# Eight transformer layers with linear attention on one core: the second norm on VectorE, the four gelu chunks together, and bias rows added by GpSimd instead of TensorE

## The reference

```
q = elu(h @ wq + bq) + 1;  k = elu(h @ wk + bk) + 1;  v = h @ wv + bv
kv = sum over tokens of k (x) v, per head;  z = 1 / (q . sum(k) + 1e-6)
att = (q . kv) * z
h = ln(h + att @ wo + bo) * g1 + be1
y = gelu(h @ w1 + c1) @ w2 + c2          # 512 hidden columns
h = ln(h + y) * g2 + be2
```

## Time and profile before

| | us |
|---|---|
| median of three runs | 1039.72 |
| the profiled execution | 1038.53 |
| its span, first to last instruction | 1036.6 |
| busy: PE / ACT / DVE / POOL | 950.8 / 777.6 / 750.1 / 301.4 |
| granted TensorE clock, mean of the span | 0.967 |

### The profile page before, as it was taken

The page is one execution under the profiler, slowest core; times in us unless marked ns, Lnnn a source line. Parts: engine busy times, 40 slices in busy tenths (PEclk is TensorE's granted clock), DMA queues, the critical chain, the costliest instruction groups (busy, mean ns, idle before and its releaser), DMA issues.

```text
span 1036.6 us, 18947 instructions
## 1 busy us (share of the span) xinstructions
PE 950.8 (92%) x5782; PEld 755.7 (73%) x5782; DVE 750.1 (72%) x2466; ACT 777.6 (75%) x1333; POOL 301.4 (29%) x299
## 2 busy tenths in 40 slices
PE   3569999999899998999899998999899999999980
PEld 2447887778777887778777886788777887787650
DVE  6867777777677767677677767677677778778646
ACT  2457888888788887888788887888788888888622
POOL 5103222322233222232233222232223222345513
PEclk9879999999999999999999999999999999999965
DMA  4100100000000100001000100001000000000002
GB/s 143 54 9 15 36 1 1 19 6 32 1 18 0 36 1 0 18 0 35 1 18 0 36 1 0 18 0 35 1 17 1 0 0 2 1 1 2 1 0 81
DMA packets 22440, 16.67 MB, mean 16 GB/s; under 512 B 3964, under 2 KB 18280, under 8 KB 22376
## 3 DMA queue, kind: packets, MB, share of 16 engines
q1 hardware_dynamic: 22376, 16.00, 5.2%
HBM read 13.89 MB, written 2.10 MB: 15 GB/s over the span
## 4 chain that ended last, share of the span: by engine, by line
PE 66%; ACT 13%; DVE 12%; issue 7%; DVEq 0%; DMA 0%; POOL 0%; POOLq 0%; ACTq 0%
PE down_ps L639 17%; PE q_ps L598 6%; PE q_ps L580 5%; PE k_ps L574 5%; ACT z_tm L767 4%; ACT L794 4%; PE att_ps L610 3%; PE up_ps L627 3%; PE up_ps L629 3%; PE up_ps L628 3%; PE small_ps L587 3%; DVE st L821 3%; PE t_ps L617 3%; PE small_ps L592 3%; PE down_ps L635 3%
## 5 line engine op out<-in xcount | busy, mean ns | idle before, releaser
L639 PEld LDWEIGHTS down_ps<-w_use,hid 128*128 128x128 f32 x2048 | 243.2, 192 | 44.9 <-issue 44.9
L639 PE MATMUL down_ps<-w_use,hid 128*128 128x128 f32 x2048 | 255.8, 278 | 0.0
L709 ACT ACTIVATE hid<-up_ps 128x512 f32<-128x512 f32 x256 | 144.8, 589 | 70.7 <-PE up_ps L629 64.5
L860 POOL TENSOR_TENSOR res_ffn<-z_tm,g_ffn 128x512 f32<-128x512 f32 x64 | 104.7, 1635 | 302.9 <-DVE z_tm L842 302.9
L853 POOL TENSOR_TENSOR res_att<-z_tm,g_att 128x512 f32<-128x512 f32 x64 | 82.4, 1288 | 351.4 <-DVE h L809 351.3
L816 DVE TENSOR_TENSOR h<-down_ps,res_ffn 128x512 f32<-128x512 f32 x64 | 44.2, 691 | 112.7 <-ACT z_tm L767 112.7
L821 DVE BATCH_NORM_STATS2 st<-h 128x6 f32<-128x128 f32 x512 | 110.9, 279 | 2.2
L627 PE MATMUL up_ps<-z_hi,w_hi 128*128 128x512 f32 x256 | 111.9, 437 | 0.4 <-DVE gate_bc L488 0.3
L767 ACT ACTIVATE z_tm<-h,shift,rstd 128x128 f32<-128x128 f32 x256 | 105.6, 483 | 2.9 <-DVE shift L834 2.1
L629 PE MATMUL up_ps<-z_lo,w_hi 128*128 128x512 f32 x256 | 101.6, 397 | 0.0
L628 PE MATMUL up_ps<-z_hi,w_lo 128*128 128x512 f32 x256 | 100.5, 393 | 0.0
(11 more groups left out here) (170 smaller groups left out, 1755.4 us busy)
## 6 DMA issues: line engine op xcount, KB each, us to landing
raw_w<-in_L_attn_W SPq DMA_DIRECT2D x16, 256.0 KB, 4.7
x_tm<-in_L_attn_x SPq DMA_DIRECT2D x4, 512.0 KB, 5.9
bias_bc<-in_L_attn_c SPq DMA_DIRECT2D x8, 256.0 KB, 4.3
out_y<-gate_tm SPq DMA_DIRECT2D x8, 256.0 KB, 2.0
raw_g<-in_L_attn_g SPq DMA_DIRECT2D x15, 64.0 KB
raw_att<-in_L_attn_Wq SPq DMA_DIRECT2D x8, 64.0 KB, 1.8
raw_att<-in_L_attn_Wk SPq DMA_DIRECT2D x8, 64.0 KB, 1.8
raw_att<-in_L_attn_Wv SPq DMA_DIRECT2D x8, 64.0 KB, 1.9
```

Source lines behind the costliest of these rows:

```text
L639: last = nc.tensor.matmul(down_ps[:, t, :], hid[:, j, t * P:(t + 1) * P], w2_use[:, j, :], start=False, stop=(j == FC - 1 and t == TT - 1))
L709: nc.scalar.activation(hid[:, j, :], up_ps[j % 2][:, :], ACT.Gelu).then_inc(s["gelu"], 1)
L860: nc.gpsimd.tensor_tensor(res_ffn[:, b % 2, :, :], z1_tm[:, :, :], g_ffn[:, :].unsqueeze(1).to_broadcast([P, TT, D]), ALU.mult).then_inc(s ...
```

## The change

There are six edits, and they depend on each other:

1. **Bias rows.** The two 2 x 512 matmuls go, with the split of the rows. The rows are now loaded by DMA to all 128 partitions. POOL adds them itself: `res_att` and `res_ffn` are each a multiply and then an add in place, so POOL has four 128 x 512 operations a period in place of two.
2. **When POOL works.** `res_att` of unit p is released by `mv1_s`, the aggregated statistics of unit p-1, no longer by `h1_s`. `res_ffn` is done for unit p-2 in period p, one period later than before, behind `res_att`, and has one buffer in place of two.
3. **Second norm.** `act_norm2` goes; `dve_norm2` does the same four instructions on DVE.
4. **DVE's order.** Both sets of `bn_stats` come first and both of `bn_aggr` after; the second half is norm1, k_phi, kvo, q_n, z1_lo, norm2, q_phi, h2.
5. **Up chunks together.** `pe_up` runs its four chunks in one piece, the third into the bank of `k_ps`, before `pe_kz`; the projection of k follows `pe_kz`.
6. **Down by tiles.** `pe_down` goes token tile by token tile with the four chunks inside, in three pieces: one tile before the denominator, one after, two after the projection of q. It waits for all four gelus.

```diff
         def pool_res_att(pool, u, b):
             z_ready(pool, u)
             if after_first(u):
-                pool.wait_ge(s["h1_s"], u)
+                pool.wait_ge(s["mv1_s"], TT * u)
             nc.gpsimd.tensor_tensor(res_att[:, :, :], z_tm[:, b, :, :], g_att[:, :].unsqueeze(1).to_broadcast([P, TT, D]),
-                                    ALU.mult).then_inc(s["t2m"], 1)
+                                    ALU.mult).then_inc(s["t2x"], 1)
+            pool.wait_ge(s["t2x"], u + 1)
+            nc.gpsimd.tensor_tensor(res_att[:, :, :], res_att[:, :, :], row_att[:, :].unsqueeze(1).to_broadcast([P, TT, D]),
+                                    ALU.add).then_inc(s["t2m"], 1)
         def pool_res_ffn(pool, u, b):
-            if after_first(u) and after_first(u - 1):
-                pool.wait_ge(s["h2_s"], u - 1)
+            if after_first(u):
+                pool.wait_ge(s["h2_s"], u)
             pool.wait_ge(s["z1n"], TT * (u + 1))
-            nc.gpsimd.tensor_tensor(res_ffn[:, b % 2, :, :], z1_tm[:, :, :], g_ffn[:, :].unsqueeze(1).to_broadcast([P, TT, D]),
-                                    ALU.mult).then_inc(s["t1m"], 1)
+            nc.gpsimd.tensor_tensor(res_ffn[:, :, :], z1_tm[:, :, :], g_ffn[:, :].unsqueeze(1).to_broadcast([P, TT, D]),
+                                    ALU.mult).then_inc(s["t1x"], 1)
+            pool.wait_ge(s["t1x"], u + 1)
+            nc.gpsimd.tensor_tensor(res_ffn[:, :, :], res_ffn[:, :, :], row_ffn[:, :].unsqueeze(1).to_broadcast([P, TT, D]),
+                                    ALU.add).then_inc(s["t1m"], 1)
...
-            if is_unit(p - 1):
-                pool_res_ffn(pool, p - 1, (b - 1) % SEQS)
+            if is_unit(p - 2):
+                pool_res_ffn(pool, p - 2, (b - 2) % SEQS)
...
         def pe_att(pe, u):
-            nc.tensor.matmul(att_flat, ones_r[:, :], row_att[:, :, :].rearrange("p t d -> p (t d)"), start=True, stop=False)
...
+        up_bank = (up_ps[0][:, :], up_ps[1][:, :], k_ps[:, :, :].rearrange("p t d -> p (t d)"), up_ps[0][:, :])
+        def pe_up(pe, u, keys):
+            pe.wait_ge(s["z1lo_s"], u + 1)
+            if after_first(u):
+                pe.wait_ge(s["gelu"], u * FC)
+            for j in range(FC):
+                if j == 2:
+                    pe.wait_ge(s["kphi"], keys)
+                if j == 3:
+                    pe.wait_ge(s["gelu"], u * FC + 1)
...
+        def pe_down(pe, u, tiles):
+            if tiles[0] == 0:
                 if after_first(u):
                     pe.wait_ge(s["h2_s"], u)
-                nc.tensor.matmul(down_flat, ones_r[:, :], row_ffn[:, :, :].rearrange("p t d -> p (t d)"), start=True, stop=False)
...
+                pe.wait_ge(s["gelu"], u * FC + FC)
+            for t in tiles:
+                for j in range(FC):
...
-        def act_norm2(act, p, v, b):
-            act.wait_ge(s["shift_s"], p)
...
+        def dve_norm2(dve, p, b):
+            dve.wait_ge(s["shift_s"], p)
+            for t in range(TT):
+                i = TT + t
+                nc.vector.tensor_scalar(z_tm[:, b, t, :], h2[:, t, :], rstd[:, i:i + 1], shift[:, i:i + 1],
+                                        ALU.mult, ALU.add).then_inc(s["z2n"], 1)
```

More of the change, by code:

```diff
@@ L111, in build @@
         res_att = sb("res_att", [P, TT, D])
-        res_ffn = sb("res_ffn", [P, 2, TT, D])
+        res_ffn = sb("res_ffn", [P, TT, D])
         h1 = sb("h1", [P, TT, D])
@@ L609, in pe_att @@
             for t in range(TT):
-                last = nc.tensor.matmul(att_ps[:, t, :], q_n[:, t * P:(t + 1) * P], kvo[:, :], start=False, stop=(t == TT - 1))
+                last = nc.tensor.matmul(att_ps[:, t, :], q_n[:, t * P:(t + 1) * P], kvo[:, :], start=True, stop=True)
             last.then_inc(s["att_done"], 1)
@@ L618, in pe_z1_transpose @@
             last.then_inc(s["t1_ps"], 1)
-        def pe_up(pe, u, chunks):
-            if chunks[0] == 0:
-                pe.wait_ge(s["z1lo_s"], u + 1)
-            for j in chunks:
-                if after_first(u) or j >= 2:
-                    pe.wait_ge(s["gelu"], u * FC + j - 1)
-                w_hi, w_lo = w1_hi[:, j * P:(j + 1) * P], w1_lo[:, j * P:(j + 1) * P]
-                nc.tensor.matmul(up_ps[j % 2][:, :], w_hi, z1_hi[:, :], start=True, stop=False)
-                nc.tensor.matmul(up_ps[j % 2][:, :], w_lo, z1_hi[:, :], start=False, stop=False)
-                nc.tensor.matmul(up_ps[j % 2][:, :], w_hi, z1_lo[:, :], start=False, stop=True).then_inc(s["up"], 1)
@@ L639, in pe_down @@
                     last = nc.tensor.matmul(down_ps[:, t, :], hid[:, j, t * P:(t + 1) * P], w2_use[:, j, :],
-                                            start=False, stop=(j == FC - 1 and t == TT - 1))
-            if chunks[-1] == FC - 1:
+                                            start=(j == 0), stop=(j == FC - 1))
+            if tiles[-1] == TT - 1:
                 last.then_inc(s["down"], 1)
@@ L761, in act_z1_hi @@
             nc.scalar.activation(z1_hi[:, :], t_ps[:, :], ACT.Identity).then_inc(s["z1hi_s"], 1)
-        def act_norm2(act, p, v, b):
-            act.wait_ge(s["shift_s"], p)
-            for t in range(TT):
-                i = TT + t
-                nc.scalar.activation(z_tm[:, b, t, :], h2[:, t, :], ACT.Identity, scale=rstd[:, i:i + 1],
-                                     bias=shift[:, i:i + 1]).then_inc(s["z2n"], 1)
         def act_state_copy(act, u, b):
@@ L815, in dve_h2, with dve_stats_of @@
                 dve.wait_ge(s["z2n"], TT * u)
-            nc.vector.tensor_tensor(h2[:, :, :], down_ps[:, :, :], res_ffn[:, b % 2, :, :], ALU.add).then_inc(s["h2_s"], 1)
-        def dve_norm_stats(dve, h, first, ready, count, st_s, mv_s, done):
+            nc.vector.tensor_tensor(h2[:, :, :], down_ps[:, :, :], res_ffn[:, :, :], ALU.add).then_inc(s["h2_s"], 1)
+        def dve_stats_of(dve, h, first, ready, count, st_s):
             dve.wait_ge(ready, count)
@@ L821, in dve_norm_stats, with dve_aggr_of @@
                 nc.vector.bn_stats(st[:, first + t, :], h[:, t, :]).then_inc(s[st_s], 1)
+        def dve_aggr_of(dve, first, st_s, mv_s, done):
             dve.wait_ge(s[st_s], TT * done + TT)
@@ L1036, in _ @@
                     load_a(sp, l)
[L1037 removed]
+                    sp.wait_ge(s["w2_ready"], l)
                     load_b(sp, l)
@@ L1138, in _ @@
                 pe_expert_up(pe, 0)
-                pe_up(pe, last, range(FC))
+                pe_up(pe, last, UNITS)
                 pe_expert_down(pe, 2)
```

151 lines of the change are left out of this document (70 added, 81 removed).

## The result

| kernel | median us | lowest to highest | runs |
|---|---|---|---|
| before | 1041.49 | 1038.48 to 1046.07 | 4 |
| changed | 1128.63 | 1123.47 to 1131.88 | 4 |

The ratio is 1.0828, with a 95% interval of 1.0765 to 1.0891: slower by 87 us. The profiled execution took 1130.56 us.

The account below looks back on a forecast made before the run. PE bound the kernel before; a DVE-POOL-DVE ring would bound the changed one at 14.8 us a period. Six looped layers add 51 us, layer 0 5, layer 7 5 and 14, draining 3: 78 on 1038.5, forecast 1117, range 1085 to 1143.

Parts of the forecast that it names:

- The mechanism: Norm1 on DVE waits for POOL's four operations, which wait for h1's statistics; ordinary periods of 14.6 to 15.0 us; chance 0.88.
- the ring: DVE's h1 addition and statistics, POOL's four operations, then DVE to the next h1 addition: 14.6 us a period, floor 14.4.
- a second ring, through PE and ACT: From norm1 through PE and ACT to k_phi and the next h1 addition: 29.5 us for two periods, 14.75 each.
- The term for b = 2: Period b = 2 of a layer: the w2 copy between POOL's pairs adds 0.6 us.
- The clock: PE's clock falling from 2.4 to 1.2 GHz in new gaps within layers would put the time far above the range.
- b = 3: Period b = 3: small operations for the next layer's affines about 0.7 us, plus POOL's row work about 1.5.
- the loop's turn, b = 7: Period in which the hardware loop turns: 2.7 us extra, on DVE and so in the ring.
- Layer 7: Last layer: four periods of 17.6 us against 14.2, adding 14; its four ordinary-like periods add 5.
- PE stays the bound: Rival, whole kernel: norm1 not held by POOL, PE sets 13.15 us a period, total 988 us; chance 0.04.
- the doubling of terms that I had put to this rule: DVE and POOL blocking on their shared port could double the b = 1 and layer 7 terms: 12 us more.

Follow-up runs that it names:

- e1: Changed kernel with POOL's two res_ffn operations ahead of its two for res_att, the w2 copy staying between the pairs; 1066.13 us.
- e3: Changed kernel with POOL's product into res_att released by the h1 addition instead of the statistics behind it; 1043.57 us.
- e11: Changed kernel with res_att released by the h1 addition and, at b = 2, the w2 copy ahead of the res_att pair; 1019.77 us.
- e2: Changed kernel with only the w2 copy of period b = 2 moved ahead of POOL's res_att pair; 1093.80 us.
- e5: Changed kernel with five small matmuls of constants put into TensorE's wait ahead of the z1 transposes; 1106.93 us.
- e12: Kernel before with only the second norm moved from ScalarE to VectorE; 1001.14 us.
- e15: Kernel before, its engine order kept, with second norm on VectorE, bias rows on GpSimd, no bias matmuls, two res_ffn buffers; 976.70 us.

## Why the prediction was right, and where its steps were off

**The mechanism was right.** The time lies in the range, 12 us above the predicted 1117. The signs of the mechanism are in the trace: norm1 released by POOL's in-place addition, POOL's four operations back to back, PE idle 1.75 to 1.88 us before the transposes. Three sizes were off: norm1 is idle for 1.45 us and not 2; ACT's busy time is down by 86.8 us and not the 106 I wrote, which was the sum of the norm's instructions as drawn; and an ordinary period that does not stand behind one of the slow clock takes 14.2 us, below my 14.6 to 15.0 and just at the value under which I had called myself wrong. e1 and e3, which open the ring in two different ways, both bring the ordinary period to 13.40.

**The ring was sized a little too long.** The terms against what they measured in the period shown: H to POOL 2.9 against 2.72, POOL's four 5.24 against 5.18, DVE from norm1 on 6.2 against 6.17, in all 14.6 against 14.21. The 14.8 that I went on with came from a second ring, through PE and ACT, which I had added up to 14.75. It was the worse sized of the two: in e1, e3 and e11, where DVE's wait for the key step is seen in nearly every period, the ordinary period is 13.4. For 48 looped periods the 0.6 us between 14.8 and 14.2 would be 29 us too much, but two other terms made up for them. That the total came out so near is in part luck.

**The term for b = 2 was mis-sized, by 5.3 us a layer.** I charged POOL's 0.6 us for the w2 copy between its pairs. With the ring's 14.2 that makes 14.8, and the period takes 19.4 to 20.8 us in the looped layers, 20.1 on average. PE now asks for w2 before kz and not before down, and the copy stands behind a pair that waits for the statistics. I had counted what the copy costs POOL, and not who waits for it, though the change moved that wait on PE. e2 put the copy first and won 35 us, 5 a layer.

**The clock was named as a risk, without a term.** I wrote that a fall within the layers would put the time far above the range. It did fall, in six of nine neighbouring periods, and by e5 it costs at least 22 us in all, 3.3 a looped layer (768.3 to 748.4 us for the six). It falls for some 3 us of a period only; that part of this stands in PE's slack is argued, not shown. So the condition was right and its price too high.

**Two terms were too large.** I had b = 3 at 2.2 us above an ordinary period, and it is 1.3; I had the loop's turn, b = 7, at 2.7, and it is 1.8 in e5, where the clock does not disturb it. Together: 8.6 us a layer predicted, 4.8 off for the ring, 5.3 on for b = 2, 3.3 on for the clock and 1.8 off for these two make 10.6, where 11.3 was measured. The other 0.7 I can't assign. Outside the looped layers the profiled executions differ by 24 us, where I had 27.

**Layer 7 was near:** three of its four long periods take 18.1 to 18.5 us and the last 16.7, where I had 17.6.

**The floor for "PE stays the bound" was wrong.** I priced it at 13.15 us a period from a PE timeline without gaps. e12 shows the same work as before's 14.1 in 13.52, and e15, without the bias matmuls, takes 13.01, so before's 14.1 was not PE's own. The rival's 988 us was near what a better order does reach (976.7), by another road.

**What remains between e11 (1020) and e15 (977)** I put down to the order of the other engines in the change: one tile of down ahead of the denominator, copies for PE behind both sets of statistics. In e11 VectorE waits 79.2 us for ScalarE's key step, and 10.6 us in e12. That is argued from the waits; no run undid this order alone, and e15 also has a second buffer for res_ffn.

## What to carry to other kernels

When a cheap engine takes over work, ask where it stands in the chain before asking whether it has time: in the change POOL was busy 37% of the time and set the pace, and in e15, busy 45%, no engine waited for it in the layers. The release of one buffer and the place of one copy alone brought 109 us (e11). A change of several parts is best taken apart even where the sum is bad: one part of this one was worth 39 us by itself, and two of them 65. And a busy TensorE without gaps in the timeline may still be waiting in small pieces; compare the distance of the same two instructions in two kernels.

## What the runs showed of the hardware

- TensorE's granted clock went from its upper level (2.4 GHz) to the lower (1.2 GHz) for some 3 us behind waits of 1.88 and 4.05 us in the changed kernel: q_ps 1.69 us for 1.02, kz 2.07 for 1.06. With five small matmuls in the wait (e5) it stayed up in the three periods shown. The changed kernel has waits of 1.75 us with no fall behind them as well (780.60), so a wait of that length doesn't always bring it about.
- An instruction of 8 columns on VectorE took 1.19 us beside GpSimd (`shift`, 776.78) and 0.17 alone in e15. The Trainium skill (SBUF — State Buffer, "SBUF: two separate sides") says that the port pair the two share is held for a whole instruction and the other engine blocks, and the trace agrees: the instruction ends at 777.97, with GpSimd's operation at 777.95. It stood in DVE's slack, so the doubling of terms that I had put to this rule did not come.
- The in-place additions, with one operand broadcast over the tiles, took 1.26 to 1.27 us alone, as the multiply does. The Trainium skill (GPSIMD Engine Reference, "Instruction dispatch") gives about 2.5 cycles an element as a floor for two inputs, an estimate of 1.07 us here; the measured time stands 0.2 us above that floor.
